# First attention stage on one core: seven of sixteen heads' probabilities transposed by DMA instead of TensorE

## The chip, the cores and the metric

The kernel runs on one core of one Trainium2 chip. The metric is the time of one execution on the device in microseconds (us). Lower is better.

## The reference, cut to what matters

Two decoder layers, each a gated cross-attention and a gated mixture of experts; the change touches the attention of layer 0 only. Sixteen batches of 112 queries and 375 keys, width 256, 16 heads of 16 columns:

```python
x = x + tanh(g_xattn[0]) * attention0(layernorm(x), ctx, mask)     # 16 heads of 16
x = x + tanh(g_ffn[0])   * experts0(layernorm(x))                  # 8 experts, best 2, dense
x = x + tanh(g_xattn[1]) * attention1(ctx, layernorm(x), mask)     # 16 heads of 64
x = x + tanh(g_ffn[1])   * experts1(layernorm(x))

def attention0(q_in, k_in, mask):          # per batch: q [112,256], k and v [375,256]
    scores = einsum('bhqd,bhkd->bhqk', q / 4, k) + (1 - mask) * -10000
    probs  = softmax(scores)               # [112, 375] per head
    return einsum('bhqk,bhkd->bhqd', probs, v)
```

## The kernel before

Three phases run one after the other. `phase_attention_small_heads` (tiles `a_...`) is layer 0, the first stage; `phase_attention_large_heads` (`b_...`) is layer 1's attention; `phase_experts` (`c_...`) is the last. Every engine has its own instruction stream, written out by hand, and they meet only at semaphores. Products in fp32 quality are made of fp16 halves: a tile has a high half (HI) and a low half (LO, the rest), and a product takes two or three matmuls.

In the first stage a batch is 16 slots, one head a slot, and the engines run it as a pipeline. In PE's slot `s` stand the scores of head `s` (into one of two banks `ps_s`), the transposes of head `s-2`, the values product of head `s-4`, and then one piece of other work from `PSLOT` (projections of batch b+1: keys in slots 0 and 1, queries in 4, values in 5 to 7) or `DSLOT` (routing and experts of batch b-1: `D_PAIRS`, 6 matmuls of 512 columns, in slots 9, 10, 12, 13). PE waits for `s_max` two heads back, so a slot can't run far ahead of the others.

- DVE: `maxima` (L827) adds the mask, writes `prob` (a ring of 4 heads) and the row's maximum; `plo` (L832) makes the low half of the transposed probabilities.
- ACT: `exps` (L691) makes the exponentials in place and their row sums (`accum_out`, a second small instruction); `phi` (L698) makes the high half of the transposed probabilities.
- PE: `transposes` (L592) turns a head's 112x375 fp32 probabilities in three blocks of 125 keys into one of two banks `ps_t`; `values` (L606) is 6 matmuls of 32 columns (HI and LO of v side by side).
- At slot 4 the attention output of the batch before is closed: `out_lo` (ACT), `read_out` (DVE, with the reciprocal of the row sums), `residual` (POOL, writes `x1`), then `stats_x1` (DVE), `deviation_x1` (POOL), `norm_x1` (DVE), from which PE's `D_XT` in slot 7 and the routing follow.
- POOL runs per batch: `deviation_x`, `residual`, `deviation_x1`, `mask_bias`, `split_queries`, `split_context`, four expert sums and `x2`.
- SP issues all DMAs of this stage but the weights' from one queue, in program order: mask, residual, tokens and context, four `k_stack` copies, eight `q_masked` copies, `clear_rows` (zeros to the later scatter buffer `xs`, 1032 KB a batch), the store of `x2`.

The second phase already turns its probabilities by DMA (`turn`, L1207): ACT writes the high half of `prob` (L1678), POOL or DVE the low half (L1286, L1784), SP issues one DMA transpose for both halves, of 8 blocks of 128 keys a head.

## Time and profile before

| | us |
|---|---|
| median of 3 runs | 1418.66 (1414.66 to 1419.71) |
| the profiled execution's own time | 1419.76 |
| its span in the profile | 1418.0 |
| first stage, whole batches in steady state (stretch 60 to 420) | 360.0: PE busy 350.7, DVE 331.5, ACT 299.4, POOL 167.4 |
| end of the first stage and start of the second (420 to 500) | 80.0: PE busy 43.4 |
| second stage (500 to 1200) | 700.0: PE busy 658.7 |
| third stage (1200 to 1418) | 218.0: PE busy 165.0 |

The profile is of one execution; its time lies 1.1 us over the median of the runs. The span is what the instructions cover, and 1.8 us of the execution lie around it. "Busy" counts overlapping instructions of an engine once. Matmuls are pipelined: each is shown longer than the distance to the next, so that distances between starts tell what a piece of PE's stream takes.

### The profile page before, as it was taken

Reading aid. Unit: us, or ns where it says so; the run is one execution under the profiler, and the core shown is the slowest. Engines: PE = TensorE matmul, PEld = TensorE weight load, DVE = VectorE, ACT = ScalarE, POOL = GpSimd, SP = SyncE. Lnnn points to the kernel's source line nnn. Section 1 sums busy time; section 2 is a strip of 40 time slices with the busy share of each in tenths; the row PEclk is TensorE's granted clock in tenths of the full one; section 3 lists DMA queues with packets and bytes.
Section 4 is the critical chain, followed back from the end, with each engine's and each line's share of the span. In section 5 each row is a group of like instructions: output and inputs, shape, how many; then the busy total and the mean of one; then the engine's idle time right before and its main releaser. Section 6 shows DMA issues by size and latency. Waiting matters only on the chain. (4 is left out here: it accounts for less than half of the span.)

```text
span 1418.0 us, 38930 instructions
## 1 busy us (share of the span) xinstructions
PE 1258.8 (89%) x13508; PEld 915.2 (65%) x13508; DVE 1092.8 (77%) x3110; ACT 1004.8 (71%) x2584; POOL 821.8 (58%) x1204
## 2 busy tenths in 40 slices
PE   5999999999987389999999999999999974489994
PEld 3788888888865145666566666656566653479994
DVE  4899999999986158888888888888888882467772
ACT  3888888788894258877878887887888771246662
POOL 3644445444454356677777777777777674146553
PEclk9999999999997699999999999999999985699997
DMA  5234333343320138787888768888877693843323
GB/s 174 79 125 121 111 108 109 109 125 95 116 63 4 37 82 147 147 154 144 154 162 158 134 154 144 156 159 159 147 146 151 139 195 59 332 133 57 59 36 75
DMA packets 304017, 175.69 MB, mean 124 GB/s; under 512 B 250234, under 2 KB 291586, under 8 KB 300720
## 3 DMA queue, kind: packets, MB, share of 16 engines
q1 hardware_dynamic: 287632, 130.94, 43.3%
q0 software_dynamic: 13168, 35.80, 10.1%
q10 hardware_dynamic: 3024, 6.47, 1.5%
q8 instruction: 110, 1.80, 0.6%
q14 instruction: 83, 0.68, 0.1%
HBM read 64.48 MB, written 41.96 MB: 75 GB/s over the span
## 5 line engine op out<-in xcount | busy, mean ns | idle before, releaser
L1653 ACT ACTIVATE b_prob<-b_prob,b_top 112x487 f32<-112x487 f32 x256 | 178.8, 698 | 28.6 <-DVE b_top L1779 26.9
L1286 POOL TENSOR_TENSOR b_halves<-b_prob,b_halves 112x487 f16<-112x487 f32 x128 | 146.9, 1148 | 82.9 <-ACT b_halves L1678 81.4
L1464 PE MATMUL b_ps_p<-w_s,b_tok_s 128*128 128x512 f16 (+1 forms) x768 | 187.7, 381 | 4.0 <-DVE b_k_s L1766 3.2
L1464 PE MATMUL b_ps_p<-b_tok_s,w_s 128*128 128x487 f16 x768 | 183.0, 376 | 6.6 <-POOL b_tok_s L1280 3.7
L1779 DVE CUSTOM_DVE_ANT_0 b_prob<-b_ps_s,b_keep 112x487 f32<-112x487 f32 x256 | 167.3, 654 | 15.5 <-PE b_ps_s L1557 12.3
L691 ACT ACTIVATE a_prob<-a_prob,a_top 112x375 f32<-112x375 f32 x256 | 156.4, 611 | 3.8 <-DVE a_top L827 2.1
L1678 ACT ACTIVATE b_halves<-b_prob 112x487 f16<-112x487 f32 x256 | 155.8, 609 | 0.6 <-issue 0.2
L827 DVE CUSTOM_DVE_ANT_0 a_prob<-a_ps_s,a_keep 112x375 f32<-112x375 f32 x256 | 138.2, 540 | 20.3 <-PE a_ps_s L583 19.6
L832 DVE TENSOR_TENSOR a_pT<-a_ps_t,a_pT 125x336 f16<-125x336 f32 x256 | 128.4, 501 | 23.5 <-ACT a_pT L698 22.5
L1572 PEld LDWEIGHTS b_ps_o<-b_v_s,b_pT 128*128 128x128 f16 (+1 forms) x3072 | 124.3, 99 | 29.7 <-DMA b_pT<-b_halves 10.2
L1572 PE MATMUL b_ps_o<-b_v_s,b_pT 128*128 128x64 f16 (+1 forms) x3072 | 135.7, 195 | 7.0 <-DMA b_pT<-b_halves 6.9
L592 PE MATMUL a_ps_t<-a_const,a_prob 112*125 112x112 f32 x768 | 127.8, 275 | 9.1 <-ACT a_prob L691 7.1
L592 PEld LDWEIGHTS a_ps_t<-a_const,a_prob 112*125 112x125 f32 x768 | 114.4, 189 | 30.6 <-ACT a_prob L691 23.3
L583 PE MATMUL a_ps_s<-a_k_stack,a_q_masked 128*112 128x375 f16 x512 | 126.5, 329 | 6.1 <-DMA a_q_masked<-a_q_s 6.1
L1464 PEld LDWEIGHTS b_ps_p<-b_tok_s,w_s 128*128 128x128 f16 x768 | 66.5, 99 | 95.7 <-issue 22.4
L1464 PEld LDWEIGHTS b_ps_p<-w_s,b_tok_s 128*128 128x128 f16 (+1 forms) x768 | 70.7, 105 | 83.5 <-DVE b_k_s L1766 12.4
L1766 DVE TENSOR_TENSOR b_k_s<-b_ps_p,b_k_s 128x487 f16<-128x487 f32 x128 | 84.5, 661 | 51.1 <-ACT b_k_s L1634 51.1
L698 ACT ACTIVATE a_pT<-a_ps_t 125x336 f16<-125x336 f32 x256 | 114.9, 449 | 11.9 <-PE a_ps_t L592 10.4
L1784 DVE TENSOR_TENSOR b_halves<-b_prob,b_halves 112x487 f16<-112x487 f32 x128 | 120.4, 940 | 0.0
L1641 ACT ACTIVATE b_v_s<-b_ps_p 128x512 f16<-128x512 f32 (+1 forms) x128 | 76.0, 594 | 53.2 <-PE b_ps_p L1464 52.2
L1774 DVE TENSOR_TENSOR b_v_s<-b_ps_p,b_v_s 128x512 f16<-128x512 f32 (+1 forms) x128 | 87.8, 686 | 31.7 <-ACT b_v_s L1641 31.7
L1557 PE MATMUL b_ps_s<-b_k_s,b_q_s 64*112 64x487 f16 x768 | 107.7, 386 | 0.3 <-DVE b_top L1779 0.3
(262 smaller groups left out, 3072.9 us busy)
## 6 DMA issues: line engine op xcount, KB each, us to landing
xs<-a_blank SPq DMA_DIRECT2D x14, 1032.0 KB, 4.2
c_w_pool<-w_split SPq DMA_DIRECT2D x8, 1600.0 KB, 10.7
b_wch_f<-in_w_experts POOLq DMA_DIRECT2D x32, 384.0 KB, 4.9
w_split<-b_wch_s POOLq DMA_DIRECT2D x32, 384.0 KB, 3.4
a_ctx_f<-in_ctxT SPq DMA_DIRECT2D x16, 375.0 KB, 3.8
a_k_stack<-a_k_s SPq DMA_DIRECT2D x64, 93.8 KB, 3.0
b_ctx_t<-in_ctx SPq DMA_DIRECT2D x16, 375.0 KB
c_xt<-xs SPq DMA_DIRECT2D x35, 129.0 KB, 2.5
```

The source lines that it names most:

```text
L583: last = pe.matmul(ps_s[h % 2][0:T, 0:C], q_masked[par][:, part, m, g * T:(g + 1) * T], k_stack[par][:, g, :], start=(part == HI), stop=(p ...
L592: last = pe.transpose(ps_t[h % 2][0:KB0, j * T:(j + 1) * T], prob[:, h % RING, j * KB0:(j + 1) * KB0], ident[0:T, 0:T])
L691: act.activation(prob[:, h % RING, :], prob[:, h % RING, :], ACT.Exp, bias=top[:, h % RING:h % RING + 1], scale=-1.0, accum_out=sums[par][ ...
L827: dve.tensor_tensor_reduce(prob[:, h % RING, :], ps_s[h % 2][0:T, 0:C], keep[par][:, :], -SCALE0, 3e38, ALU.add, ALU.min, top[:, h % RING: ...
L832: dve.tensor_tensor(pT[0:KB0, h % RING, LO, :, 0:T], ps_t[h % 2][0:KB0, 0:NB0 * T].rearrange("p (j n) -> p j n", j=NB0), pT[0:KB0, h % RIN ...
L1286: pool.tensor_tensor(halves[:, h % TURN, LO, 0:NK], prob[:, h % RING, 0:NK], halves[:, h % TURN, HI, 0:NK], ALU.subtract).then_inc(s_lo[1], 1)
L1464: last = pe.matmul(out, sta(a, k), mov(m, k), start=(k == 0 and n == 0), stop=(k == tiles - 1 and n == 2))
L1572: last = pe.matmul(ps_o[h // 8][:, col:col + D1], pT[0:k, h % TURN, a, j, :], v_s[par][0:k, m, j, h * D1:(h + 1) * D1], start=(h % 8 == 0 ...
L1653: act.activation(prob[:, h % RING, 0:NK], prob[:, h % RING, 0:NK], ACT.Exp, bias=top[:, h % RING:h % RING + 1], scale=-1.0, accum_out=sums ...
L1678: act.activation(halves[:, h % TURN, HI, 0:NK], prob[:, h % RING, 0:NK], ACT.Copy).then_inc(s_hi, 1)
L1779: dve.tensor_tensor_reduce(prob[:, h % RING, 0:NK], ps_s[h % 3][0:T, 0:NK], keep[par][:, :], -SCALE1, 3e38, ALU.add, ALU.min, top[:, h % R ...
L1784: dve.tensor_tensor(halves[:, h % TURN, LO, 0:NK], prob[:, h % RING, 0:NK], halves[:, h % TURN, HI, 0:NK], ALU.subtract).then_inc(s_lo[0], 1)
```

## The change

In the first stage heads 1, 3, ..., 13 (`BY_DMA`) are turned by DMA, the other nine (`BY_PE`) by PE as before, through one bank `ps_t` where there were two. For a head by DMA, ACT writes the high half of `prob` into `halves` (`high_half`), POOL the low half (`low_half`), and SP issues the transpose (`turn`). Blocks are 128, 128 and 119 keys. The values product of an even head stands in slot h+4 as before, that of an odd one in slot h+6 (`VSLOT`); heads 13 and 15 both stand in slot 3 of the next batch. The row sums come from a column of ones beside v (33 columns in place of 32), so `accum_out` goes; the outputs take two banks `ps_o`, read after slot 15 (heads 0 to 7) and slot 4 (heads 8 to 15). POOL's and SP's work of a batch is spread over slots by hand. The semaphores `s_turned` are shared with the second phase, which only adds an offset to its counts; loops were already written out for all batches in both kernels.

```diff
+        BY_DMA = tuple(range(1, H - 2, 2))
+        BY_PE = tuple(h for h in range(H) if h not in BY_DMA)
+        VSLOT = {s: [s - 4] if s % 2 == 0 else [s - 6] for s in range(4, H + 4)}
+        VSLOT[5] = []
+        VSLOT[H + 3] = [H - 3, H - 1]
...
+            def turn(b, h):
+                need_all(sp, settled, (s_lo, len(BY_DMA), b, BY_DMA.index(h) + 1), valued(b, h - TURN))
+                sp.dma_start(pT[:, h % TURN, :, :, 0:T].rearrange("p s j n -> p (s j) n"),
+                             halves[:, h // 2 % (TURN // 2), :, :].rearrange("p s n -> p (s n)"),
+                             transpose=True).then_inc(s_turned[h // 2 % (TURN // 2)], 16)
...
+                for s in range(H):                       # SP
+                    if s == 1 and ahead(b, 1):
+                        load_mask(b + 1, 1 - par)
+                    if s == 2 and not early(b, 2):
+                        store(b - 2)
+                    if s == 3 and ahead(b, 2):
+                        load_tokens(b + 2)
+                    if s == 5 and ahead(b, 1):
+                        stack_keys(b + 1, 1 - par)
+                    if s == 9 and ahead(b, 1):
+                        mask_queries(b + 1, 1 - par)
+                    if s == 11:
+                        clear_rows(b)
+                    if s == 13:
+                        load_residual(b)
+                    c, _, h = heads(s, 3, b, par)
+                    if h in BY_DMA and not (first(b) and s < 3):
+                        turn(c, h)
...
+            def low_half(b, h):
+                i = BY_DMA.index(h)
+                need(pool, s_hi, len(BY_DMA), b, i + 1, settled)
+                r = h // 2 % (TURN // 2)
+                pool.tensor_tensor(halves[:, r, LO, 0:C], prob[:, h % RING, 0:C], halves[:, r, HI, 0:C], ALU.subtract).then_inc(s_lo, 1)
...
+                    if s == 4 and not first(b):          # POOL
+                        residual(b - 1)
+                    if s - 2 in BY_DMA:
+                        low_half(b, s - 2)
+                    if s == 5 and not first(b):
+                        deviation_x1(b - 1)
+                    if s == 6 and ahead(b, 1):
+                        split_queries(b + 1)
...
             def transposes(b, h):
-                need(pe, s_plo, H, b, h - 1)
-                for j in range(NB0):
+                need(pe, s_plo, len(BY_PE), b, i)
+                for j in range(NA):
...
             def values(b, par, h):
-                need(pe, s_phi, H, b, h + 1)
-                need(pe, s_plo, H, b, h + 1)
+                if h in BY_DMA:
+                    need(pe, *turned(b, h))
+                else:
+                    need(pe, s_phi, len(BY_PE), b, BY_PE.index(h) + 1)
+                    need(pe, s_plo, len(BY_PE), b, BY_PE.index(h) + 1)
...
-                act.activation(prob[:, h % RING, :], prob[:, h % RING, :], ACT.Exp, bias=top[:, h % RING:h % RING + 1],
-                               scale=-1.0, accum_out=sums[par][:, h:h + 1]).then_inc(s_exp, 1)
+                act.activation(prob[:, h % RING, 0:C], prob[:, h % RING, 0:C], ACT.Exp, bias=top[:, h % RING:h % RING + 1],
+                               scale=-1.0).then_inc(s_exp, 1)
...
+            def high_half(b, h):
+                need(act, s_exp, H, b, h + 1)
...
+                act.activation(halves[:, h // 2 % (TURN // 2), HI, 0:C], prob[:, h % RING, 0:C], ACT.Copy).then_inc(s_hi, 1)
```

SP's queue in the middle of a batch, before, from the store of `x2` of the batch before to the clearing of `xs`:

```order
L347 DMA x<-a_x 112x256
L321 DMA a_keep<-in_mask 112x375
L326 DMA a_x_res<-in_x 112x256
L314 DMA a_x_in<-in_x 112x256
L316 DMA a_ctx_f<-in_ctxT 128x750
L334 DMA a_k_stack<-a_k_s 64x2x375 x4
L343 DMA a_q_masked<-a_q_s 16x2x448 x8
L352 DMA xs<-a_blank 128x2064
```

The same queue of the changed kernel, from the store of `x2` to the load of the residual. The transposes are, in order, those of head 1, of heads 3 and 5, of head 7 and of head 9:

```order
L380 DMA x<-a_x 112x256
L347 DMA a_x_in<-in_x 112x256
L349 DMA a_ctx_f<-in_ctxT 128x750
L392 DMA_TRANSPOSE a_pT<-a_halves 128x6x112
L367 DMA a_k_stack<-a_k_s 64x2x375 x4
L392 DMA_TRANSPOSE a_pT<-a_halves 128x6x112 x2
L376 DMA a_q_masked<-a_q_s 16x2x448 x8
L392 DMA_TRANSPOSE a_pT<-a_halves 128x6x112
L385 DMA xs<-a_blank 128x2064
L392 DMA_TRANSPOSE a_pT<-a_halves 128x6x112
L359 DMA a_x_res<-in_x 112x256
```

The transpose of head 7 now stands behind all eight `q_masked` copies, and that of head 9 behind the clearing of `xs`; before, nothing but the store and the loads of later batches stood behind either.

POOL's queue before, from the normalised output of the batch before (`o_n`, in `residual`) to the splits of queries and context:

```order
L431 TENSOR_TENSOR a_o_n<-a_o_f,a_rsum_t 112x256
L435 TENSOR_TENSOR a_x<-a_o_n,a_x_b 112x256
L403 TENSOR_SCALAR a_var<-a_mv 112x1
L405 TENSOR_TENSOR a_rstd<-a_var,a_neg_half 112x1
L416 TENSOR_SCALAR a_keep<-a_keep 112x375
L421 CAST a_q_s<-a_q_f 128x448
L423 TENSOR_TENSOR a_q_s<-a_q_f,a_q_s 128x448
L396 CAST a_ctx_s<-a_ctx_f 128x750
```

POOL's queue of the changed kernel over the same piece; the `a_halves` rows are the low halves of heads 3, 5 and 7:

```order
L494 TENSOR_TENSOR a_o_n<-a_o_f,a_rsum_t 112x256
L498 TENSOR_TENSOR a_x<-a_o_n,a_x_b 112x256
L458 TENSOR_TENSOR a_halves<-a_prob,a_halves 112x375
L463 TENSOR_SCALAR a_var<-a_mv 112x1
L465 TENSOR_TENSOR a_rstd<-a_var,a_neg_half 112x1
L481 CAST a_q_s<-a_q_f 128x448
L483 TENSOR_TENSOR a_q_s<-a_q_f,a_q_s 128x448
L458 TENSOR_TENSOR a_halves<-a_prob,a_halves 112x375
L446 CAST a_ctx_s<-a_ctx_f 128x750
L458 TENSOR_TENSOR a_halves<-a_prob,a_halves 112x375
```

The low half of head 3 now stands between `x1` and the deviation, and that of head 5 behind the deviation and the split of the queries; the mask's scaling moved ahead of this piece.

PE's stream in slots 13, 14 and 15 of the changed kernel (scores, transposes, values, other work); before, each slot had its three transposes (L592):

```order
L664 MATMUL a_ps_s<-a_k_stack,a_q_masked 112x375 x2
L694 MATMUL a_ps_o<-a_v_s,a_pT 128x33 x6
L579 MATMUL a_ps_p<-a_we_s,a_x1T 112x512 x6
L664 MATMUL a_ps_s<-a_k_stack,a_q_masked 112x375 x2
L674 MATMUL a_ps_t<-a_const,a_prob 128x112 x3
L694 MATMUL a_ps_o<-a_v_s,a_pT 128x33 x6
L647 MATMUL a_ps_p<-a_be_s,a_cwT 112x256 x3
L664 MATMUL a_ps_s<-a_k_stack,a_q_masked 112x375 x2
L694 MATMUL a_ps_o<-a_v_s,a_pT 128x33 x6
```

The first L694 row is head 7's values (slot 13), the last is head 9's (slot 15); each now waits for its DMA.

## Rows read from the trace of the kernel before

**Rows 1.** A stretch of the first stage: busy us (instructions) of PE, PEld, DVE, ACT, POOL; clock; DMA share; GB/s

```profile
60.00:420.00 360.00, 350.72 (x3684) 290.71 (x3682) 331.54 (x1144) 299.37 (x923) 167.44 (x240) 1.00 0.35 106
```

**Rows 2.** Tile `xs`, 60 to 420: clearing DMAs, duration ns min/median/max, first and last start

```profile
L352 SPq DMA_DIRECT2D xs<-a_blank x13: 582/583/970, 70.5 to 380.2; - x13
...
DMA to landing us min/median/max: 2.5/4.2/4.5
```

**Rows 3.** Timeline of PE, slots 13 to 15 of one batch: start, us, line

```profile
227.95 0.48 PE L583 MATMUL a_ps_s<-a_k_stack,a_q_masked 128*112 128x375 f16 x2
228.27 0.48 PE L592 MATMUL a_ps_t<-a_const,a_prob 112*125 112x112 f32 x3
228.59 0.31 PE L606 MATMUL a_ps_o<-a_v_s,a_pT 125*128 125x32 f16 x6
228.75 1.48 PE L499 MATMUL a_ps_p<-a_we_s,a_x1T 128*112 128x512 f16 x6
230.06 0.48 PE L583 MATMUL a_ps_s<-a_k_stack,a_q_masked 128*112 128x375 f16 x2
...
231.21 0.48 PE L583 MATMUL a_ps_s<-a_k_stack,a_q_masked 128*112 128x375 f16 x2
```

**Rows 4.** Groups by line and form, 60 to 420: busy us, mean ns | idle before

```profile
L832 DVE TENSOR_TENSOR a_pT<-a_ps_t,a_pT 125x336 f16<-125x336 f32 x221 | 110.7, 501 | 15.0 <-ACT a_pT L698 14.3
...
L698 ACT ACTIVATE a_pT<-a_ps_t 125x336 f16<-125x336 f32 x221 | 99.0, 448 | 8.0 <-PE a_ps_t L592 6.6
...
L691 ACT ACTIVATION_READ_ACCUMULATOR a_prob<-a_prob,a_top 112x1 f32 x221 | 44.5, 201 | 0.0
```

**Rows 5.** The page's groups of the second stage: both halves of 487 keys

```profile
L1286 POOL TENSOR_TENSOR b_halves<-b_prob,b_halves 112x487 f16<-112x487 f32 x128 | 146.9, 1148 | 82.9 <-ACT b_halves L1678 81.4
...
L1678 ACT ACTIVATE b_halves<-b_prob 112x487 f16<-112x487 f32 x256 | 155.8, 609 | 0.6 <-issue 0.2
```

**Rows 6.** Timeline of one batch: its first scores, and POOL in slots 5 to 7

```profile
206.10 0.50 PE L583 MATMUL a_ps_s<-a_k_stack,a_q_masked 128*112 128x375 f16 x2
...
214.95 0.72 POOL L435 TENSOR_TENSOR a_x<-a_o_n,a_x_b 112x256 f32<-112x256 f32 x1
...
216.77 0.55 POOL L405 TENSOR_TENSOR a_rstd<-a_var,a_neg_half 112x1 f32<-112x1 f32 x1
...
217.99 0.56 POOL L421 CAST a_q_s<-a_q_f 128x448 f16<-128x448 f32 x1
218.63 1.04 POOL L423 TENSOR_TENSOR a_q_s<-a_q_f,a_q_s 128x448 f16<-128x448 f32 x1
```

**Rows 7.** Tile `b_pT`, SP's queue, second stage: DMA transposes, issue ns, landing

```profile
L1207 SPq DMA_TRANSPOSE b_pT<-b_halves x256: 1221/1228/2960, 526.0 to 1176.2; - x128
...
DMA to landing us min/median/max: 2.9/3.1/8.2
```

**Rows 8.** Timeline of SP's queue, the same batch as rows 6

```profile
219.69 5.11 SPq L343 DMA_DIRECT2D a_q_masked<-a_q_s  x8
224.85 0.58 SPq L352 DMA_DIRECT2D xs<-a_blank  x1
```

**Rows 9.** SP's queue in the second stage: a transpose behind a 375 KB load

```profile
889.50 0.47 SPq L1187 DMA_DIRECT2D b_ctx_t<-in_ctx  x1
...
890.93 1.91 SPq L1207 DMA_TRANSPOSE b_pT<-b_halves  x1
...
DMA to landing us min/median/max: 5.6/5.6/5.6
```

**Rows 10.** DMA queue totals, 500 to 1200: packets, MB, share of 16 engines

```profile
q1 hardware_dynamic: 250194, 69.63, 60.4%
```

**Rows 11.** Timeline of PE in the last batch: a wait and what follows it

```profile
429.03 0.64 PE L552 MATMUL a_ps_p<-a_const,a_xn 112*128 112x112 f32 x2 [2.56 <-DVE a_xn L803]
429.46 0.83 PE L583 MATMUL a_ps_s<-a_k_stack,a_q_masked 128*112 128x375 f16 x2
...
432.92 2.79 PE L499 MATMUL a_ps_p<-a_we_s,a_x1T 128*112 128x512 f16 x6
```

More of the change, by code:

```diff
@@ L40 @@
 KB0, NB0 = 125, 3
+KA, NA = 128, 3
+CP = NA * KA
 SCALE0 = D0 ** -0.5
@@ L196, in phase_attention_small_heads @@
         ps_s = [bank(f"ps_s{i}") for i in range(2)]
-        ps_t = [bank(f"ps_t{i}") for i in range(2)]
-        ps_o = bank("ps_o")
+        ps_t = bank("ps_t")
+        ps_o = [bank(f"ps_o{i}") for i in range(2)]
         ps_p = [bank(f"ps_p{i}") for i in range(3)]
-        s_blank = sem("blank")
         s_cleared = sem("cleared")
@@ L488, in _ @@
             run_batches(pool, body)
+            residual_bias(B - 1)
             residual(B - 1)
             deviation_x1(B - 1)
-            sum_experts(B - 1)
+            for j in range(E // 2):
+                add_expert(B - 1, j)
+            finish(B - 1)
         @block.tensor
@@ L609, in values @@
                 last.then_inc(s_pv, 1)
-            def drain(b, par):
-                for s in range(4):
-                    for lag, stage in ((2, transposes), (4, values)):
-                        h = H + s - lag
-                        if h < H:
-                            stage(b, h) if lag == 2 else stage(b, par, h)
             def body(b, par):
@@ L620, in body @@
                     scores(b, par, s)
-                    if not (first(b) and s < 2):
-                        c, _, h = heads(s, 2, b, par)
+                    c, _, h = heads(s, 2, b, par)
+                    if h in BY_PE and not (first(b) and s < 2):
                         transposes(c, h)
-                    if s == 5:
-                        values(b, par, 0)
-                    if s != 4 and not (first(b) and s < 4):
-                        values(*heads(s, 4, b, par))
+                    for h in VSLOT.get(s + H, []):
+                        if not first(b):
+                            values(b - 1, 1 - par, h)
+                    for h in VSLOT.get(s, []):
+                        values(b, par, h)
                     if ahead(b, 1):
@@ L641, in _ @@
             run_batches(pe, body)
-            drain(B - 1, 1)
+            for s in range(H, H + 4):
+                if s - 2 < H:
+                    transposes(B - 1, s - 2)
+                for h in VSLOT[s]:
+                    values(B - 1, 1, h)
             for k in range(DI):
@@ L754, in body @@
                         c, _, h = heads(s, 2, b, par)
-                        phi(c, h)
+                        if h in BY_PE:
+                            phi(c, h)
+                    if s - 1 in BY_DMA:
+                        high_half(b, s - 1)
+                    if s == H - 1:
+                        out_lo(b, 0)
                     if ahead(b, 1) and P_Q in PSLOT.get(s - 1, []):
@@ new lines, in plo, with read_out @@
+                dve.tensor_tensor(pT[:, h % TURN, LO, :, 0:T],
+                                  ps_t[:, 0:NA * T].rearrange("p (j n) -> p j n", j=NA),
+                                  pT[:, h % TURN, HI, :, 0:T], ALU.subtract).then_inc(s_plo, 1)
+            def read_out(c, i):
+                group = slice(8 * i, 8 * i + 8)
+                out = ps_o[i][0:T, 0:8 * VW].rearrange("p (h d) -> p h d", h=8)
+                need(dve, s_pv, H, c, max(VALUES.index(h) for h in range(8 * i, 8 * i + 8)) + 1)
+                need(dve, s_olo, 2, c, i + 1)
+                dve.reciprocal(rsum[:, group], out[:, :, 2 * D0]).then_inc(s_rsum, 1)
+                need(dve, s_on, 1, c, 0)
+                dve.tensor_tensor(o_f[:, group, :], out[:, :, 0:D0], o_lo[:, group, :], ALU.add).then_inc(s_oread, 1)
+                if i:
+                    need(dve, s_rsum, 2, c, 2)
+                    dve.tensor_scalar(rsum_t[:, :], rsum[:, :], tanhs[0:T, 0:1], None, ALU.mult).then_inc(s_rsumt, 1)
@@ L924, in body @@
                         c, _, h = heads(s, 2, b, par)
-                        plo(c, h)
+                        if h in BY_PE:
+                            plo(c, h)
+                    if s == H - 1:
+                        read_out(b, 0)
                     if ahead(b, 1) and s == 0:
@@ L1104, in phase_attention_large_heads @@
         s_lo = [sem("lo_even"), sem("lo_odd")]
-        s_turned = [sem(f"turned{i}") for i in range(RING)]
         s_pv = sem("pv")
@@ L2263, in build_program @@
         s_rows = ctx.enter_context(nc.semaphore("rows"))
+        s_turned = [ctx.enter_context(nc.semaphore(f"turned{i}")) for i in range(4)]
         with nc.sbuf_tensor("w1_s", [128, 2, WKV + WQ + WOUT], F16) as w1_s:
```

214 lines of the change are left out of this document (116 added, 98 removed).

## The prediction

> **What bounds the kernel now.** I read the stretches first. In the steady part of the first stage PE is busy 97% of the time, DVE 92%, ACT 83%, POOL 47%, at full clock, with the DMA engines 35% busy [rows 1]. A batch repeats every (380.2 - 70.5) / 12 = 25.8 us, by the clearing DMA that SP issues once a batch [rows 2]. So TensorE sets the pace with DVE close behind, and SP and the DMAs have room. The timeline of PE tells what its pieces really take, from start to start: scores 0.32 us (227.95 to 228.27), a head's three transposes 0.32 (to 228.59), its values 0.16 (to 228.75), an expert pair 1.31 (to 230.06), slot 14 with its bias 1.15 (to 231.21) [rows 3]. The "busy" 0.48 of the transposes would overstate what their removal gives.
>
> **What goes.** Seven of sixteen heads lose their transposes on PE: 7 x 0.32 = 2.2 us a batch [rows 3]. They also lose `plo`, 7 x 0.50 = 3.5 us of DVE, and `phi`, 7 x 0.45 = 3.1 us of ACT; ACT drops 16 accumulator reads, 16 x 0.20 = 3.2 us shown, though these overlap their neighbours and free less [rows 4]. If nothing else moved, PE would stay the slowest engine and a batch would take 25.8 - 2.2 = 23.6 us. [...] `read_out` in two halves costs DVE a few tenths, covered by the 3.5 us it loses.
>
> **What is added, by engine.** No trace shows a 375-key half made in this stage. For POOL's low half the nearest rows are 112x487 at 1.15 us and the 448-column split of q at 1.04 [rows 5, 6]; by columns 375 gives 0.88 from the first and 0.87 from the second, and I take 0.9: 7 x 0.9 = 6.3 us a batch, POOL 47% to about 72%. ACT's high half is 0.61 us at 487 keys [rows 5], so 0.47 to 0.61 here; 7 x 0.5 = 3.5 us, about what `phi` gives back. The DMA transpose costs SP 1.23 us to issue and lands 3.1 us after its issue began, at 1024 columns [rows 7]. Here it has 768 columns: by size 0.92, by count 1.23; I take 1.0 for the issue and 2.9 for the landing (bounds 2.6 and 3.1). All of queue q1 in the second stage is 0.604 x 700 x 16 / 256 = 26 engine-us a transpose [rows 10], at most 1.7 us of all sixteen engines, at 768 columns 1.2: seven make 8.7 us a batch, and the DMA engines go from 35% to about 70%. Neither POOL nor SP nor the DMAs run out of throughput. The single bank `ps_t` matters only where PE turns neighbours (14, 15, 0): two waits of `plo` that the key projections in slots 0 and 1 cover; without that cover about 1 us each.
>
> **What decides is latency.** A head by DMA has six slots from scores to values. Most have enough; head 7 has not, and head 9 behind it. I follow one batch from its first scores (206.10 = 0) [rows 6].
>
> 1. `x1` of the batch before ends at 215.67, at 9.6. The path to it (values of 15 in slot 3, `out_lo`, `read_out`, `residual`) is as long as before, so I keep 9.6.
> 2. POOL now makes the low half of head 3 behind it, 0.9: 10.5. Then the deviation, which takes 0.8 (0.55 shown from 216.77 and its small forerunner): 11.3. The split of q takes 217.99 to 219.67 = 1.7: 13.0. Then the low half of head 5, 0.9, and 0.1 for the signal: 14.0.
> 3. SP waits for that, since the transpose of head 5 is next in its queue: issue 1.0, 15.1 with the semaphore. Then the eight `q_masked` copies, 5.15 us [rows 8]: 20.25. Only then the transpose of head 7, which lands 2.9 later: **23.15**.
> 4. PE wants it in slot 13, 0.32 behind that slot's scores. Before, that was 227.95 + 0.64 - 206.10 = 22.5; with five of the odd slots shorter by 0.32 it would be 20.9. So PE stands about 2.2 us, all that the seven transposes gave.
> 5. From there PE has head 7's values 0.16, the pair 1.31, slot 14 at 1.15, and the scores of slot 15 at 0.32: 26.1 when it wants head 9.
> 6. Head 9's transpose is issued at 20.25 + 1.0 + 0.6 = 21.85, behind the clearing of `xs`, 1032 KB that land 4.2 us after issue [rows 2], at 25.45. How far a transpose waits for data issued ahead of it must be bounded: not at all, then it lands at 24.75 and PE doesn't wait; as one behind a 375 KB load in the second stage did, 5.6 us [rows 9], then at 27.45; or as long as the clearing plus its own 1.2 us, 26.65. I take the last, because it lies between and adds two measured pieces. With the 0.16 of its values slot 15 ends at 26.8.
>
> [...]
>
> A batch thus takes 26.8 us where it took 25.8; the bounds of step 6 give 26.3 and 27.6. Fourteen batches (1 to 14) have both neighbours: 14 x 1.0 = 14 us. Batch 0 has no residual chain ahead of its splits and the last no `q_masked` copies; I cost them at nothing together, since their slots are light and ACT paces them, and what ACT saves in accumulator reads it spends on halves. Against the profiled execution: 1419.8 + 14 = 1433.8; that execution is 1.1 over the median of the runs, so **1433 us**. The likeliest case's own range is 14 x 0.5 = 7 to 14 x 1.8 = 25 more: 1426 to 1444.
>
> **Rivals.**
>
> - *The turned heads are in time, and TensorE's saving stays* (faster). It needs the low half of head 5 about 2 us earlier, by 12, or the copies issued while SP waits. For it: steps 1 to 3 keep a chain measured under an engine mix that will be lighter; DVE and ACT each lose work. Against it: 5.15 us of issue and 2.9 of landing are fixed, and 15.1 us + 8.05 can't meet 20.9. Full saving: 14 x 2.2 = 31, 1388 us. Half of it, when POOL's chain is 1.5 us shorter and head 9 doesn't queue: 24.8 us a batch, 1405. Together 0.25.
> - *It comes out even*: the stall at head 7 eats the saving and head 9 waits for nothing (the lower bound of step 6, with step 2 half a us shorter): 25.8 to 26.0 a batch, 1419 to 1421. It decides whether the transfers queue. 0.2.
> - *My chain* (slower), 0.45.
> - *The clock falls too* (slower). [...] If every stall did this, a pair and slot 14 would cost at least 2.4 more a batch: 29.2 us, 1433 + 14 x 2.4 = 1467. 0.1.
>
> A further way to lose: DVE may write `prob` for head h+4 only when POOL has the low half of head h. Head 9's maximum wants head 5's low half at 14.0, and its scores come at about 14; one us later there and DVE, then PE, stand by as much. It is in the upper part of the range.
>
> **The numbers.** A difference within 0.5%, 7 us, is about what a measurement of this kernel can't tell from none. Faster 0.25 and even 0.2 are the first two cases, slower 0.55 the last two. The range reaches from the half saving less some, 1396, to most of the clock's case, 1456: below lies the full saving, above a clock that falls in each batch, less than 2 in 10 together.
>
> **What would show each step.** Right: clearing DMAs 26.3 to 27.6 us apart; PE waiting for DMA `a_pT<-a_halves` before the values in slots 13 and 15, 2.2 and 0.5 us a batch; SP's queue waiting for POOL's low half of head 5 at 14 us, then 5.1 us of `q_masked`; a landing of head 9's transpose near 4.8 us while the others take about 3; PE busy near 85%. Wrong: batches 23.6 apart, no wait for DMA, low half of head 5 done by 12. The low half at 1.1 us or more, or a transpose that takes 5 us to land in an empty queue, would move me up; the saving would be lost in another place if PE waited instead for DVE's `norm_x1` in slot 7.

## The result, and the profile after

| | before | after |
|---|---|---|
| median of 3 runs, us | 1418.66 (1414.66 to 1419.71) | **1464.05** (1458.93 to 1466.65) |
| the profiled execution | 1419.76 | 1466.65 |

The ratio is 1.0317, 95% interval 1.0273 to 1.0361: 3.2% slower. Forecast was slower by 1.0%, 1433 us, at most 1456: the direction held, the size did not.

Where in the program the time comes in is read from two tiles, one used once a batch and one once a head. First PE's transpose of the combine weights (`a_cw`, once a batch), in the kernel before and then after (instruction durations in ns, first and last start in us):

```profile
L559 PE MATMUL a_ps_p<-a_const,a_cw x16: 261/296/297, 70.3 to 460.1; 112*128 112x112 f32 x16
```

```profile
L640 PE MATMUL a_ps_p<-a_const,a_cw x16: 262/287/290, 77.0 to 508.3; 112*128 112x112 f32 x16
```

Fifteen intervals take 389.8 us before and 431.3 after: 26.0 and 28.75 us a batch, +41.5 us together; the first comes 6.7 us later. Then SP's queue in the second stage, for tile `b_pT` of the changed kernel (before: [rows 7]):

```profile
L1313 SPq DMA_TRANSPOSE b_pT<-b_halves x256: 1221/1227/2323, 574.6 to 1224.1; - x128
```

It starts 48.6 us later (526.0 before) and ends 47.9 later: the second stage takes as long as it did. The loss is in the first stage, 41.5 in its batches and 6.7 ahead of them.

The steady stretch of the changed kernel, same columns as [rows 1], then the clearing DMAs with their landing, as in [rows 2], and the new transposes with theirs:

```profile
80.00:440.00 360.00, 295.22 (x3104) 223.03 (x3104) 285.66 (x974) 253.45 (x640) 220.15 (x302) 0.99 0.68 145
```

```profile
L385 SPq DMA_DIRECT2D xs<-a_blank x13: 582/583/1887, 79.1 to 423.7; - x13
...
DMA to landing us min/median/max: 4.5/4.8/7.1
```

```profile
L392 SPq DMA_TRANSPOSE a_pT<-a_halves x88: 1202/1212/2788, 79.8 to 437.5; - x88
...
DMA to landing us min/median/max: 2.6/3.3/7.0
```

PE is busy 82% where it was 97%, DVE 79% (92%), the mean clock is 0.99 (1.00), the DMA engines' share went from 35% to 68%. A clearing comes every (423.7 - 79.1) / 12 = 28.7 us. No engine is at its limit: what grew is waiting. PE's waits over the same 360 us (us in total, times, longest):

```profile
PE a_ps_o L694 <- DMA a_pT<-a_halves: 39.4, 34, 3.2
...
PE a_ps_p L640 <- DVE a_cw L1007: 12.0, 12, 1.2
PE a_ps_t L674 <- ACT a_prob L777: 6.9, 12, 0.7
```

Per batch of 28.7 us (12.5 in the stretch) that is 3.15 us for transposes, 0.95 for the combine weights, 0.55 for the exponentials: 4.65 us. A listed wait begins where the instruction before it is shown to end, and that is some 0.16 us behind the point where the next would have started (scores are shown as 0.48 us and are 0.32 apart), so the 4.6 waits a batch cost 0.7 more. The kernel before has 0.4 us a batch of such waits, for the exponentials. That leaves 5.0. Less the 2.24 us of PE work removed and 0.3 for the other nine heads' transposes, now 0.29 apart and not 0.32: +2.5, of the 2.75 to 2.9 measured.

The remaining 0.4 is the clock, which the mean of 0.99 hides. Three times between 80 and 440, from about 112, 149 and 200 us, the granted clock was 0.5 for 3.4 us; in the kernel before it was so in the last batch only (428.9 to 435.8). The third time, in the columns of [rows 1]: PE stands, then works at a clock of 0.5.

```profile
197.50:200.60 3.10, 0.00 (x0) 0.00 (x0) 0.91 (x3) 0.61 (x2) 1.47 (x3) 1.00 0.88 269
200.60:204.00 3.40, 3.39 (x15) 1.97 (x16) 0.00 (x0) 0.40 (x2) 0.00 (x0) 0.53 1.07 215
204.00:208.00 4.00, 3.80 (x40) 2.68 (x39) 3.78 (x15) 3.39 (x9) 2.41 (x4) 0.98 0.49 134
```

In the middle row an expert pair takes 2.58 us from start to start where it takes 1.31 at a clock of 1.00, and the scores behind it 0.63 where they take 0.32: each spell costs 1.7 us, the three 5 us. Waits for a transpose of 2.1, 3.1 and 3.2 us went ahead of them; one of 2.6 us, at 86, was followed by none.

The waits for DMA stand mainly in three places. By slot, averaged over PE's timeline from 60 to 420, they are 1.44 us in slot 13 (head 7), 0.82 in slot 15 (head 9) and 0.53 in slot 1 (head 11, nearly all in every second batch). Timelines of one batch, whose first scores start at 233.19. SP's queue and PE:

```profile
244.53 2.92 SPq L392 DMA_TRANSPOSE a_pT<-a_halves  x2
...
245.32 0.90 POOL L458 TENSOR_TENSOR a_halves<-a_prob,a_halves 112x375 f16<-112x375 f32 x1
...
247.54 6.13 SPq L376 DMA_DIRECT2D a_q_masked<-a_q_s  x8
...
253.78 1.23 SPq L392 DMA_TRANSPOSE a_pT<-a_halves  x1
...
255.05 0.58 SPq L385 DMA_DIRECT2D xs<-a_blank  x1
...
255.74 1.99 SPq L392 DMA_TRANSPOSE a_pT<-a_halves  x1
...
256.50 0.32 PE L694 MATMUL a_ps_o<-a_v_s,a_pT 128*128 128x33 f16 x6 [1.40 <-DMA a_pT<-a_halves]
...
260.40 0.32 PE L694 MATMUL a_ps_o<-a_v_s,a_pT 128*128 128x33 f16 x6 [0.82 <-DMA a_pT<-a_halves]
```

Head 5's low half ends at 246.22, 13.0 us after the first scores. Head 7's transpose is issued at 253.78, behind the eight copies, and its values start at 256.50; head 9's is issued at 255.74, and its values start at 260.40, 4.66 us later. This is the chain of the prediction, link by link.

The wait in slot 11 is not in the prediction. The same batch, DVE and POOL beside each other, and PE behind them:

```profile
247.78 1.60 POOL L451 TENSOR_TENSOR a_ctx_s<-a_ctx_f,a_ctx_s 128x750 f16<-128x750 f32 x1
...
248.22 1.19 DVE L989 CAST a_place_f<-a_place 112x8 f32<-112x8 uint32 x1
...
251.03 0.90 POOL L458 TENSOR_TENSOR a_halves<-a_prob,a_halves 112x375 f16<-112x375 f32 x1 [1.65 <-ACT a_halves L793]
251.19 0.76 DVE L1007 TENSOR_TENSOR a_cw<-a_picked 112x8 f32<-112x8 f32 x1
...
252.09 0.29 PE L640 MATMUL a_ps_p<-a_const,a_cw 112*128 112x112 f32 x1 [0.66 <-DVE a_cw L1007]
```

Two DVE instructions on 8 columns take 1.19 and 0.76 us. Each ends when POOL's does: 248.22 + 1.19 = 249.41 against 247.78 + 1.60 = 249.38, and 251.95 against 251.93. Their groups before, and then after (busy us, mean ns):

```profile
L885 DVE CAST a_place_f<-a_place 112x8 f32<-112x8 uint32 x14 | 2.4, 172 | 0.5
...
L903 DVE TENSOR_TENSOR a_cw<-a_picked 112x8 f32<-112x8 f32 x14 | 2.3, 167 | 0.5
```

```profile
L989 DVE CAST a_place_f<-a_place 112x8 f32<-112x8 uint32 x12 | 14.4, 1196 | 0.4
L1007 DVE TENSOR_TENSOR a_cw<-a_picked 112x8 f32<-112x8 f32 x12 | 8.5, 707 | 0.4
```

Instructions that took 0.17 us take 1.20 and 0.71: 1.56 us a batch ahead of PE's slot 11. What the trace shows is the two common ends above; by what means POOL's instruction holds DVE's, it does not show.

This wait is large, but it does not set the pace. Head 7's values start when its transpose has landed, and that comes from POOL's and SP's queues: 23.31 us after the first scores here, with the wait in slot 11, where the prediction had 23.15 without it. PE would only have stood longer in slot 13.

### The profile page after: what moved, and what is told of

Its sections match the earlier page's. It is cut to its first block and busy times, and to the rows that moved or that the text cites. A ratio compares the mean times of both kernels' runs of the same rounds, so it can differ in the third digit from the quotient of the medians.

```text
span 1464.8 us, 38091 instructions
## 1 busy us (share of the span) xinstructions
PE 1231.7 (84%) x13172; PEld 864.8 (59%) x13172; DVE 1070.7 (73%) x3030; ACT 987.8 (67%) x2344; POOL 920.4 (63%) x1320
## 5 line engine op out<-in xcount | busy, mean ns | idle before, releaser
L1759 ACT ACTIVATE b_prob<-b_prob,b_top 112x487 f32<-112x487 f32 x256 | 178.9, 699 | 28.9 <-DVE b_top L1885 27.3
L458 POOL TENSOR_TENSOR a_halves<-a_prob,a_halves 112x375 f16<-112x375 f32 x112 | 100.7, 899 | 115.6 <-ACT a_halves L793 115.4
L664 PE MATMUL a_ps_s<-a_k_stack,a_q_masked 128*112 128x375 f16 x512 | 131.1, 340 | 5.9 <-DMA a_q_masked<-a_q_s 5.9
L694 PE MATMUL a_ps_o<-a_v_s,a_pT 128*128 128x33 f16 (+1 forms) x1536 | 77.5, 180 | 51.6 <-DMA a_pT<-a_halves 51.3
L1570 PEld LDWEIGHTS b_ps_p<-w_s,b_tok_s 128*128 128x128 f16 (+1 forms) x768 | 70.7, 105 | 83.5 <-DVE b_k_s L1872 12.5
L694 PEld LDWEIGHTS a_ps_o<-a_v_s,a_pT 128*128 128x128 f16 (+1 forms) x1536 | 71.0, 98 | 73.9 <-DMA a_pT<-a_halves 68.0
L579 PE MATMUL a_ps_p<-a_we_s,a_x1T 128*112 128x512 f16 x384 | 100.4, 401 | 2.1 <-DVE a_acc L977 0.2
```

Of the source, the lines that this page charges most:

```text
L664: last = pe.matmul(ps_s[h % 2][0:T, 0:C], q_masked[par][:, part, m, g * T:(g + 1) * T], k_stack[par][:, g, :], start=(part == HI), stop=(p ...
L694: last = pe.matmul(ps_o[h // 8][:, col:col + VW - 1], pT[0:r, h % TURN, part, j, :], v_s[par][0:r, j, h, 0:VW - 1], start=(h % 8 == 0 and ...
L1570: last = pe.matmul(out, sta(a, k), mov(m, k), start=(k == 0 and n == 0), stop=(k == tiles - 1 and n == 2))
L1759: act.activation(prob[:, h % RING, 0:NK], prob[:, h % RING, 0:NK], ACT.Exp, bias=top[:, h % RING:h % RING + 1], scale=-1.0, accum_out=sums ...
```

## The experiments

"A batch" is the mean distance between first scores in the steady part, and a wait "in slot n" the mean of PE's own waits there, per batch. Every ratio is to the kernel before on the same chip. The granted clock matters for what follows; this is how long it was 0.5 in each profiled execution between 80 and 400 us:

| | before | changed | e1 | e2 | e3 | e4 | e5 | e8 | e13 | e14 | e15 | e16 | e17 | e18 |
|---|---|---|---|---|---|---|---|---|---|---|---|---|---|---|
| us at clock 0.5 | 0 | 10 | 27 | 0 | 27 | 25 | 0 | 7 | 10 | 0 | 17 | 7 | 3 | 0 |

**e1: the eight query copies behind head 7's transpose.**

```diff
-                    if s == 9 and ahead(b, 1):
+                    if s == 11 and ahead(b, 1):
                         mask_queries(b + 1, 1 - par)
```

> The changed kernel with one move: SP issues the eight q_masked copies behind the transpose of head 7 instead of ahead of it. Theory (SP's queue delays head 7): PE's wait before the values of slot 13, 1.5 us a batch in the changed kernel, goes; the transpose of head 9 now stands behind the copies and the clearing, so slot 15 waits more, by about 1 us. Net 0 to 1 us a batch less, 1448 to 1464 us. Rival (the transposes are slow because the DMA engines are loaded, whatever the order): the wait in slot 13 stays at 1 us or more and the time is 1464.

1472.60 us, ratio 1.0386 [1.0344, 1.0429]. The wait in slot 13 is gone, and slot 15 waits 3.39 us in place of 0.82: the copies now stand ahead of head 9's transpose. The copies' 5 to 6 us of issue delay whatever head stands behind them. The forecast, 1464 at most, missed that slot 15 would lose more than slot 13 gains, and the clock, at 0.5 for 27 us of 320.

**e2: the clearing of `xs` in slot 15** (`if s == 15: clear_rows(b)`), behind head 9's transpose.

> The changed kernel with one move: the 1032 KB clearing of xs is issued behind the transpose of head 11 (slot 15) instead of between those of heads 7 and 9. Theory (a transpose waits for data issued ahead of it in its queue): slot 15's wait, 0.8 us a batch, goes and part of it comes back in slot 1 or 3 for head 13: 1452 to 1460 us. Rival (order in the queue costs only the 0.6 us of issue): slot 15's wait falls by 0.6 at most and head 13 is not later; 1456 to 1464.

1449.56 us, 1.0246 [1.0206, 1.0287], 27.7 us a batch. Slot 15's wait for DMA is gone: by the medians 14.5 us less than the changed kernel, by the ratios 10, from moving one 1032 KB transfer. Part of it is the clock, which does not fall here.

**e3: both.**

> Both moves: q_masked copies behind head 7's transpose, the clearing behind head 11's. Theory (the two together hold what the changed kernel lost to SP's queue): waits in slots 13 and 15 fall from 2.3 us a batch to under 0.8, 1435 to 1446 us. Rival (what was lost is lost on the engines, DVE slowed by POOL above all): the waits for the DMA go but the batch stays near 27.5 us, 1455 or more.

1453.56 us, 1.0243 [1.0219, 1.0268]. The forecast of 1435 to 1446 missed: no wait in slot 13, 0.1 in slot 15, and yet no more than e2 gave. Batches now alternate: 26.5 and 30.5 us. The long ones have this in slot 1 (PE's timeline, head 11's values):

```profile
256.12 0.32 PE L694 MATMUL a_ps_o<-a_v_s,a_pT 128*128 128x33 f16 x6 [3.23 <-DMA a_pT<-a_halves]
```

In every second batch ACT issues a 512 KB load (`load_next`, `a_next_f`) in slot 0 from its own queue, beside head 11's transpose on SP's. Behind such a wait the clock fell: here it was 0.5 from 257 to 261, and eight times 3.4 us in 320. By the 1.7 us of a spell in the changed kernel that is an estimated 14 us, which e2 did not pay.

**e4: the context's low half on POOL in slot 12 instead of 10.**

> The changed kernel with one move on POOL: the low half of the context is made in slot 12 instead of slot 10, where it lay beside DVE's routing. Theory of contention (DVE's cast of the places takes 1.19 us in place of 0.17 while POOL subtracts): that cast is back under 0.3 us and the slot 11 wait of PE falls from 1.1 to about 0.5 us. If the wait for head 7 in slot 13 is what holds the batch, PE only waits longer there and the time stays 1460 to 1464; if the contention holds it, 14 x 0.6 = 8 us less, 1455.

1468.22 us, 1.0340 [1.0299, 1.0381]. DVE's groups:

```profile
L1003 DVE TENSOR_SCALAR a_picked<-a_const,a_place_f,a_w_top 112x8 f32<-112x8 f32 x24 | 31.5, 1355 | 0.4
L989 DVE CAST a_place_f<-a_place 112x8 f32<-112x8 uint32 x12 | 2.1, 172 | 0.4
L1007 DVE TENSOR_TENSOR a_cw<-a_picked 112x8 f32<-112x8 f32 x12 | 2.0, 167 | 0.4
```

The cast is back at 0.172 us, but `picked`, which now runs beside the subtraction, went from 0.317 to 1.355, and slot 11 waits 2.0 us (0.95 in the changed kernel). The stretch follows POOL's instruction from one DVE instruction to another: shown. What it costs in time is another matter. As slot 11's wait grew by 1.1, slot 13's fell from 1.4 to 0.1, and the run is 4 us from the changed kernel, with 25 us at clock 0.5 against 10: PE stood in the one place or in the other, as the expectation said it would if head 7 holds the batch.

**e5, e6, e7: all heads by PE, the single bank and the column of ones kept; then POOL's seven low halves made beside it for nobody; then the seven DMA transposes too, into a tile that nobody reads.** The values of head h stand in slot h+4.

```diff
-        BY_DMA = tuple(range(1, H - 2, 2))
+        BY_DMA = ()
```

> The changed kernel with the DMA part undone: all 16 heads are turned by PE through the one bank, their values in slot h+4; the column of ones, the blocks of 128 keys, the two output banks and the spread order of POOL and SP stay. Theory (the loss is the turned heads' path alone): 26.0 to 26.6 us a batch, of which the one bank's waits are up to 0.6: 1416 to 1430 us. Rival (the one bank or the new order of POOL's work costs as much as the DMAs): over 1435.

> As the run with all heads by PE, and POOL makes in addition the seven low halves a batch, at their places, from prob and a tile of zeros, for nobody: no high halves on ACT, no DMA. It measures POOL's added work and what it does to DVE. Theory of contention: DVE's cast of the places and its small routing instructions are stretched as in the changed kernel, and a batch is 0.5 to 1.2 us longer than with all heads by PE: 7 to 17 us more. Rival (POOL's work is hidden): within 3 us of it.

> As the run before, and SP issues all seven DMA transposes a batch of those halves, into a tile that nobody reads; PE waits for none. It measures the transfers without the waits. Theory (what counts is how late the turned heads are, not that the transfers run): within 5 us of the run without the DMAs. Rival (SP's queue or the DMA engines delay the k_stack, q_masked and mask loads): 10 us or more over it.

1497.61, 1501.69 and 1501.32 us; ratios 1.0559 [1.0538, 1.058], 1.0596 [1.0573, 1.0619], 1.0584 [1.0563, 1.0604]. My expectation of e5 missed by 70 us. The waits in it, 80 to 440:

```profile
PEld a_ps_t L671 <- ACT a_prob L774: 42.4, 47, 1.0
PE a_ps_t L671 <- DVE a_pT L930: 40.7, 80, 0.6
```

With one bank, each head's transposes wait until DVE has read the head before: 3.5 us of PE's waits a batch, and 1.4 for the exponentials, in a batch of 31.0, when all heads are neighbours. In the changed kernel only 14, 15 and 0 are, and it has next to none of these waits. So e5 is no undoing of the turning by DMA. Beside e5, seven low halves cost 4 us and the seven transfers nothing that shows (-0.4 us). DVE's cast takes 0.172 us in e6 and e7, so the stretch expected of e6 did not come: in a batch this long POOL's work falls elsewhere. That is weak evidence, since e5 has 5 us of waits a batch to hide them in; it speaks against a dearth of POOL's or the DMAs' time, not against a wait for them.

**e8: four moves together:** e3's two, the 512 KB loads in slot 5, and the context's low half behind the first expert sum in POOL's queue.

> The changed kernel with four moves: q_masked copies behind head 7's transpose, clearing behind head 11's, ACT's load of the next stage's weights (512 KB, every second batch) in slot 5 instead of slot 0, and the low half of the context behind the first expert sum. Theory (in the run with two moves every second batch had 3.3 us of wait in slot 1, by that load; and DVE's routing is stretched by POOL): long batches fall from 30.5 to about 26.5 and all lose 0.3 to 0.8 more: 25.8 to 26.4 us a batch, 1418 to 1428 us. Rival (the wait in slot 1 comes from the clearing behind head 11): no better than 1450.

1448.82 us, 1.0205 [1.0175, 1.0236], 27.2 us a batch; the forecast of 1418 to 1428 missed by 21. Slot 1 and slot 13 are free of waits; slots 3, 7, 9 and 15 have 0.56, 0.81, 0.54 and 0.32 for transposes, slot 11 0.51 for DVE. Seven heads can't all be placed out of the way of the copies, the clearing and the load by these moves.

**e9 to e12: two banks for PE's transposes again.** For that the outputs go back to one bank and the sums to the accumulator: e9 the changed kernel so, e10 with all heads by PE, e11 e8 so, e12 with heads 1, 3, 5 and 13 by DMA. e12 also has two of e8's moves, the 512 KB load in slot 5 and the context's low half behind the first expert sum; the copies and the clearing stay where the changed kernel has them.

```diff
-                need(pe, s_plo, len(BY_PE), b, i)
+                need(pe, s_plo, len(BY_PE), b, i - 1)
                 for j in range(NA):
-                    last = pe.transpose(ps_t[:, j * T:(j + 1) * T],
+                    last = pe.transpose(turning(b, h)[:, j * T:(j + 1) * T],
```

> The changed kernel with two banks for PE's transposes again, one bank for all outputs, and the row sums by the exponentials' accumulator as before; the turning by DMA, POOL's and SP's orders stay. Theory (latency of the turned heads decides, the single bank is a side cost): in the changed kernel PE waits 0.5 us a batch in slot 4 for ACT and little else that the bank explains, so a batch goes from 28.6 to about 28.0 us and the run takes 1450 to 1460 us. Rival (the single bank is the main loss, since it cost some 5 us a batch where all sixteen heads went through it): most of the 2.6 us a batch comes back, 1425 us or less.

> All sixteen heads turned by PE, through two banks, sums by the accumulator; only the blocks of 128, 128 and 119 keys and POOL's and SP's work spread over slots are left of the change. If the single bank is what made all-by-PE 5 us a batch slower, a batch is back at 25.8 to 26 us and the run takes 1412 to 1425 us. Rival (the spread order of POOL and SP or the blocks carry a part of the loss): 1440 us or more, with PE waiting for POOL's or SP's products.

> The kernel with all four moves (query copies behind head 7's transpose, clearing in slot 15, the 512 KB loads in slot 5, the context's low half behind the first expert sum), with two banks as well. Latency theory: the waits left are for transposes (slots 3, 7, 9, 15) and for the combine weights, the bank gives 0.3 to 0.6 us a batch: 1440 to 1446 us. Rival (single bank): below 1420 us.

> Two banks, and only heads 1, 3, 5 and 13 turned by DMA, those whose transposes stand in SP's queue ahead of the query copies and the clearing or long behind them; heads 7, 9 and 11 go by PE. The 512 KB loads stand in slot 5, the context's low half behind the first expert sum. If the loss of the change is the heads whose transposes queue, plus POOL beside DVE's routing, PE's saving of 4 x 0.32 = 1.3 us a batch shows: 24.5 to 25.2 us a batch, 1397 to 1408 us. Rival (turning by DMA costs by itself, by POOL's and ACT's halves, whichever heads it takes): 1420 us or more.

1479.27, 1447.66, 1449.27 and 1432.45 us; ratios 1.0426 [1.0402, 1.0451], 1.0214 [1.0190, 1.0238], 1.0215 [1.0183, 1.0246], 1.0103 [1.0082, 1.0123]. All lie over their forecasts, and all have a wait in slot 4 (1.25, 1.51, 0.79, 1.27 us) that is in good part my own: with one output bank, head 0's values wait until the outputs of the batch before are read, and I had left them in slot 4. (In e9, 0.7 of it is the wait for exponentials, which the changed kernel has too.) The kernel before has head 0's values in slot 5. These four are confounded; the next four have them in slot 5.

```diff
+        VSLOT[4], VSLOT[5] = [], [0] + VSLOT[5]
```

**e13 (as e9), e14 (as e10), e15 (as e11), e16 (as e12).**

> As the changed kernel with two banks for PE's transposes, one for outputs and sums by the accumulator, but head 0's values in slot 5, as the kernel before has them, so that the 1.25 us wait in slot 4 of the last such kernel goes. Theory (latency of turned heads and POOL beside DVE make the loss): 29.85 - 1.25 = 28.6 less 0.3 to 0.5 for the bank, 28.1 to 28.6 us a batch, 1455 to 1464 us. Rival (the single bank carries half of the loss or more): 27.3 us a batch or less, 1445 us or less.

> All sixteen heads by PE through two banks, head 0's values in slot 5. Theory (the order of POOL's and SP's work and the blocks of 128 keys cost nothing): 27.94 - 1.5 - 0.6 = 25.8 us a batch, 1412 to 1422 us. Rival (they carry part): 1430 us or more.

> The four moves with two banks, head 0's values in slot 5. From 27.8 us a batch with a wait of 0.8 to 1.0 in slot 4: 26.8 to 27.0 us, 1433 to 1440 us by the latency theory, since waits for transposes stay in slots 3, 7, 9 and 15 (2.0 us together). Rival: below 1420 us.

> Heads 1, 3, 5 and 13 by DMA, two banks, head 0's values in slot 5. From 26.7 us a batch less the 1.27 of slot 4: 25.2 to 25.6 us, 1402 to 1415 us, faster than before, if the loss is due to those heads that queue. Rival (the wait moves to slots 0, 5 or 7 and turning costs by itself): 1420 us or more.

| | us | ratio |
|---|---|---|
| e13 seven heads by DMA | 1470.13 | 1.0368 [1.0344, 1.0393] |
| e14 all by PE | 1422.02 | 1.0028 [1.0015, 1.0042] |
| e15 seven heads, four moves | 1453.83 | 1.0244 [1.0217, 1.0272] |
| e16 four heads | 1429.06 | 1.0082 [1.0056, 1.0108] |

e14 and e13 differ only in how seven heads are turned, with their halves and the slots of their values: 1422 against 1470. The order of POOL's and SP's work and the blocks of 128 carry 4 us of the loss, turning seven heads by DMA 48. e14's 4 us have a visible cause:

```profile
PE a_ps_p L634 <- DVE a_xn L901: 10.3, 14, 2.6
```

```profile
L901 DVE TENSOR_SCALAR a_xn<-a_x,a_mv,a_rstd 112x256 f32<-112x256 f32 x14 | 17.1, 1225 | 0.0
```

DVE's `a_xn` lies beside POOL's split of the queries and takes 1.23 us (0.85 before), and PE waits for it in slot 7. The cast, in the same order of POOL's work but without low halves, takes 0.172: it is the low halves that push POOL's subtraction into the routing.

e13 is 6 us over the changed kernel, in which a single bank stands: the bank is not what costs there, and the two-bank form, if anything, is the slower (the intervals of the two ratios overlap). The rival of the single bank, alive after e5, falls. e13 is 6 us over its forecast too. e15 missed its forecast by 14 us: waits for transposes in slots 3, 7, 9 and 15 are 2.0 us a batch, as expected, but slot 0 and slot 4 wait 0.27 and 0.39 for ACT as well.

e16 is slower than before, 14 us over its forecast, and alternates: short batches of 25.2 us, long ones of 26.2 to 29.3. A long one, SP's queue, ACT's queue and PE:

```profile
239.60 1.20 SPq L396 DMA_TRANSPOSE a_pT<-a_halves  x1
240.32 0.33 ACTq L809 DMA_DIRECT2D a_next_f<-in_w  x1
240.91 2.68 SPq L371 DMA_DIRECT2D a_k_stack<-a_k_s  x4
...
246.54 0.34 PE L695 MATMUL a_ps_o<-a_v_s,a_pT 128*128 128x32 f16 x6 [2.50 <-DMA a_pT<-a_halves]
```

Head 1's transpose is issued at 239.60 and its values start at 246.54, 6.9 us later. The DMA issues of that stretch (238 to 250: count, KB, median us to landing) name what was beside it:

```profile
a_next_f<-in_w ACTq DMA_DIRECT2D x1, 512.0 KB, 5.9
a_ctx_f<-in_ctxT SPq DMA_DIRECT2D x1, 375.0 KB, 3.5
...
a_pT<-a_halves SPq DMA_TRANSPOSE x3, 6.1
```

The 375 KB load of the context, 1.7 us ahead of the transpose in SP's own queue, is there in every batch; the 512 KB load only in the long ones.

**e17: e16 with that load in slot 10** of its batch (but for the last such batch), where no transpose is under way. **e18: e17 with head 13 by PE as well** (heads 1, 3 and 5 by DMA).

```diff
-                    if par == 0 and not first(b) and s == 5:
+                    if par == 0 and not first(b) and s == (10 if ahead(b, 2) else 0):
                         load_next(b * (NLOAD // 2) - NLOAD)
```

> As the kernel with heads 1, 3, 5 and 13 by DMA and two banks, but ACT issues its 512 KB load in slot 10 of every second batch in place of slot 5, where no transpose is on its way. Theory (head 1's transpose waits for that load's data in slot 7 of every second batch, 1.0 to 3.1 us): all batches take 25.2 us, as every second one does there, and the run 1403 to 1413 us, below the kernel before. Rival (the transposes are late for another reason): slot 7 keeps its wait, 1425 us or more.

> As the kernel beside it, with head 13 turned by PE too (heads 1, 3 and 5 by DMA). PE has 0.32 us a batch more, but slot 15 is as long as before, so that the 0.6 us wait for ACT in slot 0 should go: 25.0 to 25.4 us a batch, 1403 to 1415 us. If the waits for ACT in slots 0 and 4 are ACT's own pace, they stay and it is 0.3 us a batch slower than the kernel beside it.

e17: 1412.05 us, 0.9966 [0.9942, 0.9991]. e18: **1402.22 us, 0.9891 [0.9870, 0.9912]**, the best of all. In e17 slot 7's wait for DMA (0.95 us a batch in e16) is gone and batches take 25.0 to 25.5 us, but for one of 28.5 in which the clock fell; one load moved by five slots is worth 17 us, by the ratios. It is the only edit between the two: that the load delays the transpose, though another engine issues it, is shown. The transposes landed after 6.1 us beside the load (median of three), against a median of 2.7 in e17 (80 to 400) and in e18. By what means it delays them no trace shows.

e18's steady stretch (80 to 440), its clearing DMAs, its transposes and their landing:

```profile
80.00:440.00 360.00, 329.98 (x3554) 263.24 (x3551) 316.72 (x1107) 300.41 (x924) 209.50 (x288) 0.97 0.49 123
```

```profile
L389 SPq DMA_DIRECT2D xs<-a_blank x13: 582/586/590, 69.1 to 369.1; - x13
```

```profile
L396 SPq DMA_TRANSPOSE a_pT<-a_halves x42: 1202/1229/1867, 81.4 to 414.1; - x42
...
DMA to landing us min/median/max: 2.6/2.7/5.0
```

and PE's wait for them, and DVE's cast:

```profile
PE a_ps_o L694 <- DMA a_pT<-a_halves: 1.5, 5, 0.6
```

```profile
L984 DVE CAST a_place_f<-a_place 112x8 f32<-112x8 uint32 x14 | 2.4, 171 | 0.5
```

(369.1 - 69.1) / 12 = 25.0 us a batch, 0.8 less than before, where three heads' transposes are 0.96 of PE. The transposes land in 2.7 us and PE waits 1.5 us for them in 360; POOL has no low half beside the routing and the cast takes 0.171. The 0.55 us wait for ACT in slot 0 of e17 went with head 13, as expected. e18 is 10 us faster than e17 with less work taken from PE; part of that is the clock.

How much of e18's 1.1% is the three heads' is not isolated. e18 also has the 512 KB load in slot 10 and the context's low half behind the first expert sum, and no run has all heads by PE with these two. In e14, which has neither, PE waits for neither the load nor the routing, so they should bring little there by themselves; and three heads by DMA also change where POOL works, DVE's `a_xn` taking 0.60 us in e18.

## Why the prediction was off in size

Step by step, in its own numbers:

- **Steps 1 to 3** (x1, POOL's chain, SP's queue) held, each earlier or later by a us: in the batch above x1 ended 8.8 us after the first scores (9.6 forecast), head 5's low half at 13.0 (14.0), and the copies took 6.1 us (5.1 to 6.1 over all batches, 5.15 forecast). Issue of a transpose was 1.21 us, not the 1.0 I took: the bound "by count". The 0.1 for the signal was an estimate: head 5's transpose was issued at 246.24, 0.02 behind the end of its low half. Head 7's values started at 23.3 (23.15): that this fits so well is partly luck, an earlier low half against longer copies.
- **Step 4** has a slip: before, slot 13's values stood behind its own transposes, 0.32, which go too. PE wants head 7 at 20.6 and not 20.9, and would stand 2.5 us and not 2.2. The sum is not touched, since it runs over the landing at 23.15. PE's listed waits are 1.44 in slot 13 and 0.95 in slot 11, together what was forecast for slot 13 alone.
- **Step 6** held in kind: head 9's values started 4.66 us after its issue (4.8 forecast for the landing), and slot 15 waits 0.82 (0.5). e1 and e2 confirm each cause by moving it away: the copies, and the clearing. But in the quiet batches named below its issue came 22.4 to 22.7 us after the first scores, not at 21.85, because copies and transposes take longer to issue.
- **The step that failed is "I follow one batch", taken for all fourteen, and through SP's queue only.** Four batches are like it, those with first scores at 233.19, 289.56, 345.25 and 401.99: they take 27.3 to 27.5 us, 0.6 over the 26.8, nearly all of it step 6's late issue. The three between them take 28.2 to 29.3, 1.4 more. In these ACT's 512 KB load, which the prediction put at nothing, delays head 11: PE waits 0.9 to 1.6 us in slot 1, and x1 and all behind it come later. The five before, from 86.43 on, average 29.4: there single waits reach 3.2 us, and the clock is 0.5 for 3.4 us three times. Averaged: 0.6 for the issue, 0.7 for the load, 0.5 for the five, the 1.8 to 1.9 us a batch that are missing.
- **"What is added, by engine"** was wrong in its method. POOL's low halves were costed as POOL's time, and "neither POOL nor SP nor the DMAs run out of throughput" was taken as enough. They push POOL's work beside DVE's routing and hold it up: a wait of 0.95 us a batch in slot 11, forecast as nothing. The trace of before already had the sign: DVE's `a_xn` beside POOL took 733 ns on 256 columns, and 437 in the changed kernel. In the changed kernel this wait is hidden ahead of head 7's (e4), so it is not part of the missing time.
- **"The key projections cover"** the waits at the neighbours 14, 15, 0: PE waits 0.5 us in slot 4 for exponentials, since the slots before it are shorter; small, and not named. It lies ahead of head 7's chain, as slot 11's does.
- **The ends at nothing**: the first combine weights come 6.7 us later.

The sum: 14 x 1.0 was forecast; 41.5 (15 intervals) and 6.7 were measured. That both are slower is the forecast's mechanism, not luck; three tenths of the size was caught.

**The rivals.** "The turned heads are in time" fails for seven heads. For three it holds: PE waits 1.5 us in 360 for them in e18, whose batch is 0.8 us shorter than before. "It comes out even" needed head 9 not to queue; e2 shows that this is worth 10 to 14.5 us, and would not have done. "The clock falls too" was put as a fall at every stall or none, at 0.1. Its 2.4 us a batch, from which the range's upper end comes, is a pair and slot 14 (1.31 + 1.15 [rows 3]) taken once more. The trace of before has this once: behind the wait of 2.56 us the pair took 2.79 us in place of 1.48 [rows 3, 11], at a clock of 0.50. No run shows it at every stall. It came in between: three times in the changed kernel, some 5 us, and eight times in e1 and in e3. The range's upper end of 1456 had room for this, but not together with the load and the ends.

Left open: why head 7's transpose took 4.4 and 6.1 us from issue to use in two of the early batches, with the same transfers in its queue, why the clock fell after some long waits and not after others, and how the 6.7 us ahead of the steady part arise. No run isolated these.

## What to carry to other kernels

Moving work from a busy engine to a DMA replaced throughput by latency here, 2.24 us of PE's work a batch by 3.15 us of its waits for transposes, so cost it head by head: for each turned head list what stands ahead of its transfer in *every* queue that issues DMAs, and turn only those with slack; three well-placed heads, with one load and one POOL instruction moved, gave 1.1% where seven cost 3.2%. Follow more than one batch: the load that came every second batch was in none of the steps. A wait that one edit removes can reappear in the next slot, so before you price it, ask what it hides behind. Read the clock in windows of a few us, since a mean of 0.99 held three spells of 3.4 us at 0.5. When work moves to POOL, look in the timeline for the short DVE instructions it will lie beside, since these grew four- to sevenfold (0.17 us to 0.71 and 1.20, in e4 0.32 to 1.36) while POOL, busy 220 of 360 us, itself had time. Before undoing one part of a change, check what the other parts presuppose: all heads by PE with a single bank cost 5.6%, and with two banks 0.3%.

## What the runs showed of the hardware that was not expected

A DMA transpose of six blocks takes as long to issue as one of eight (1.21 against 1.23 us), so size saves nothing there. It lands 2.6 us after issue at the least and 2.7 in the median of e18; its values started 4.7 us after issue with 1032 KB ahead of it in its own queue, and it landed after 6.1 with 512 KB beside it from another queue. The same DVE cast on 8 columns took between 0.17 and 1.42 us in the changed kernel; with POOL's subtraction moved away from it (e4) it took 0.172. In the changed kernel the granted clock was 0.5 for 3.4 us after waits of PE of 2.1, 3.1 and 3.2 us, and after one of 2.6 it was not.
